# Half of the result blocks loaded into buffers outside the expert weights, one buffer per block

## The chip, the cores and the metric

The kernel runs on one core of a Trainium2 chip. The metric is the device time of one execution in microseconds (us); the time of the kernel before is the median of three runs, 806.97 us (805.11, 806.97 and 813.48). The core has a matrix engine (PE), a vector engine (DVE), an activation engine (ACT), GpSimd (POOL) and SyncE (SP). SP, ACT and POOL issue DMAs, which all run on the core's 16 DMA engines.

## The reference

Input is x of 16 batches x 256 tokens x 128 values, f32. The layer has two halves:

```
x = x + ga * attention_and_mlp(layernorm(x) * (1 + ca) + sa)
h = layernorm(x) * (1 + cb) + sb
scores  = sigmoid(h @ gate_w.T);  ids = top 4 of (scores + e_bias), of 32 experts
topk_w  = scores[ids] / sum(scores[ids])
out[t]  = sum over the 4 experts e of  topk_w * ((silu(h @ w1[e]) * (h @ w3[e])) @ w2[e])
x = x + gb * out
```

The change touches only the last two lines: the sum over the four expert results of each token, its product with gb, and the addition to x.

## The kernel before, in words

Attention, the dense MLP and the routing run first, batch after batch. For each of its four experts a token's row is scattered to `xs` in device memory, sorted by expert, and the rows are then worked off in 192 tiles of 128 rows by the **expert loop**: 48 steps (`XSTEPS`) of four tiles. The batches fall into two parts: tiles of batches 0 to 11 come first (`FIRST_PART`), 32 steps, then those of batches 12 to 15, 16 steps.

In a step SP loads four tiles (`load_pair`, L478, started by `load_four`, which waits at L491 until a buffer of two steps ago is free), PE transposes them (L1282), multiplies by w1 and w3 (L1290, weights in `w13`, which lies in the tensor `BIAS`), ACT and DVE form silu(g)*u (L939, L1818), PE transposes (L1299) and multiplies by w2 (L1308, weights in `w2e`), and DVE weights the result and puts it into one of 64 slots of `YQ` (L1832, L1834). Each of the four slots counts up the semaphore `y_ev`. POOL scatters the slots to `ys` in device memory (L739), 128 rows of 512 bytes each, 128 scatters in all; the first 96 hold everything of batches 0 to 11. Their landings count the semaphores `yst0` to `yst3`. In `ys` the four results of a token lie side by side, so a batch is one block of 512 KB, 4 KB for each partition and token pair.

**The end of the kernel**, which the change is about, is the loop over the 16 batches (blocks) b that stands on four engines at once, each taking them in the order 0 to 15:

- SP, L510 to L520: after its last load for the expert loop it waits until `y_ev` says that the last slot is written, then for the scatters that hold the first 12 blocks, and loads block after block into a buffer `G[b % 10]`. From block 12 on it also waits for the last scatters (L517), from block 10 on for the buffer's release (`g_free`, L519).
- PE, L1352 to L1367: waits for the end of the loop too. It adds the four results for 11 of the 16 blocks (all but 2, 5, 8, 11 and 14) by four accumulating matmuls with the identity, 256 columns each, in f32; each is recorded as two. For the blocks 0 to 5 of its own it then waits for its own matmuls before it releases the buffer (L1365).
- DVE, L1865 to L1886: for a PE block it multiplies the PSUM bank by gb (L1870) and adds it to X (L1886). For the other five it adds the four results itself (L1877, L1879), multiplies (L1883) and adds to X (L1886).
- ACT, L986 to L990: sends each finished batch of X to the output, 128 KB a batch, and waits for all of them.

The ten buffers `G` are six in `w13` and four in `w2e`: both hold expert weights that the loop reads until its last step. Other memory of that size is idle in the loop: the modulation rows `moda` and gate rows `gates[0]` of the first half, the buffer `early` and the hidden buffer `hid[0]`; some of them serve as rows for the scatter to `xs` and are free once that has landed, which SP waits for at L503.

Of the kernel before, what the change touches and what calls it, by code (L numbers as in the profile page):

```python
# [28 lines left out]
NB, SEQ, D = 16, 256, 128  # L29
# [5 lines left out]
NE, TOPK, INNER = 32, 4, 96  # L35
# [16 lines left out]
XG = 4  # L52
# [4 lines left out]
XSTEPS = XTILES // XG  # L57
# [22 lines left out]
def build(nc, x, ln1_w, Wq, Wk, Wv, rel_bias, scale, Wo, ln2_w, W1, W2, gate_w, w1, w3, w2, e_bias, c, wmod,  # L80
          onehot, out):
    ctx = ExitStack()
    with ctx:
        def sb(name, shape, dt=F32):
            return ctx.enter_context(nc.sbuf_tensor(name, shape, dt))

        def sem(name):
            return ctx.enter_context(nc.semaphore(name))

        def dram(name, shape):  # L90
# [11 lines left out]
        ident = sb("ident", [P, P])  # L102
# [26 lines left out]
        gates = [modb[:, i * NB * D:(i + 1) * NB * D].rearrange("p (b d) -> p b d", b=NB) for i in range(2)]  # L129
        moda_flat = modb[:, 2 * NB * D:]  # L130
# [7 lines left out]
        w13 = BIAS[:, :, :].rearrange("p u w -> p (u w)")  # L138
        w2r = sb("w2e", [P, NE, D])
# [9 lines left out]
        early = sb("early", [P, 2 * SEQ + UW])  # L149
# [34 lines left out]
        hid_flat = [hid[i][:, :, :].rearrange("p c t -> p (c t)") for i in range(2)]  # L184
# [55 lines left out]
        yidx = sb("yidx", [P, SLOTS + YGROUP], I32)  # L240
        tag = [sb(f"tag{i}", [P, XG, 2]) for i in range(4)]
        G = [f[:, i * TPB * TOPK * D:(i + 1) * TPB * TOPK * D].rearrange("p (t k d) -> p t k d", t=TPB, k=TOPK)
             for f, n in ((w13, 6), (w2r[:, :, :].rearrange("p e d -> p (e d)"), 4)) for i in range(n)]
        acc = [V[0][:, :, :, :].rearrange("p t h s -> p (t h s)")[:, i * SEQ:(i + 1) * SEQ].rearrange(
            "p (t d) -> p t d", t=TPB) for i in range(4)]

        def summed_on_pe(b):
            return b % 3 != 2
# [3 lines left out]
        names = """ld_c ld_wm ident_ready ld_x0 ld_x ld_w ld_v ld_b ld_e pool_c pool_s pool_n   # L252
# [9 lines left out]
             cnt_pe zero_ready zero_done  x_rows0 x_rows1 x_rows2 x_rows3  t_ready wr_t ld_t   # L262
            xt_pe xt_ev gu_pe sg_act a_dve at_pe at_act y_pe y_ev xg_ev yz yst0 yst1 yst2 yst3 pad_ready pad_done settled
             acc_s sum_s acc_ready ost0 ost1 ost2 ost3 ks_pe scat0 scat1 scat2 scat3 scat4 scat5 scat6 scat7 h2_copies""".split()
        names += [f"g_rows{i}" for i in range(len(G))] + [f"g_free{i}" for i in range(NB - len(G))]
        s = {n: sem(n) for n in names}
        block = ctx.enter_context(nc.Block())

# [4 lines left out]
        def bank(b, n=512, m=0):  # L273
            return PS[:, b, m:m + n]
# [90 lines left out]
        def tok(buf, b, t=0, n=1):  # L365

            return buf[:, bass.ds(b * TPB + t, n), :]
# [6 lines left out]
        def _(sp):  # L374
# [132 lines left out]
            with sp.Fori(early_fours, XSTEPS // 4 - 1) as four:  # L507
                load_four(four * 4)

            sp.wait_ge(s["y_ev"], XG * (XSTEPS + 2))  # L510
            ysv = ys[0:YROWS, :].rearrange("(b p t k) d -> b p (t k d)", b=NB, t=TPB, p=P)
            for b in range(NB):
                r = b % len(G)
                if b in (0, FIRST_PART):
                    slots = (FIRST_PART if b == 0 else NB) * TPB * TOPK
                    for g in range(SLOTS // 16):
                        sp.wait_ge(s[f"yst{g}"], 16 * 16 * (slots // SLOTS + (1 if g < slots % SLOTS // 16 else 0)))  # L517
                if b >= len(G):
                    sp.wait_ge(s[f"g_free{r}"], 1)  # L519
                sp.dma_start(G[r].rearrange("p t k d -> p (t k d)"), ysv[b]).then_inc(s[f"g_rows{r}"], 16)  # L520


        @block.gpsimd
# [470 lines left out]
        def _(pe):  # L994
# [13 lines left out]
            for j in range(2):  # L1008
                last = pe.transpose(bank(0, NB, j * NB), mrow[:, 3 + j, :], ident[0:NB, 0:NB])
# [137 lines left out]
            with pe.Fori(0, 5) as two:  # L1147
                b = two * 2 + 1
# [205 lines left out]
            n = 0  # L1354
            for b in range(NB):
                if summed_on_pe(b):
                    r = b % len(G)
                    pe.wait_ge(s[f"g_rows{r}"], 16 * (b // len(G) + 1))
                    if n >= 4:
                        pe.wait_ge(s["acc_s"], n - 4 + 1)  # L1360
                    for k in range(TOPK):
                        last = pe.matmul(bank(n % 4, SEQ), ident[:, :], G[r][:, :, k, :], start=(k == 0), stop=(k == TOPK - 1))
                    last.then_inc(s["ks_pe"], 1)
                    if b + len(G) < NB:
                        pe.wait_ge(s["ks_pe"], n + 1)  # L1365
                        pe.sem_inc(s[f"g_free{r}"], 1)
                    n += 1  # L1367


# [1 line left out]
        def _(dve):  # L1371
# [227 lines left out]
            with dve.Fori(0, 5) as two:  # L1599
                b = two * 2 + 1  # L1600
# [259 lines left out]
            for n in range(4):  # L1860
                i = XSTEPS - 4 + n
# [2 lines left out]

            n = m = 0  # L1865
            for b in range(NB):
                r, o = b % len(G), acc[b % 4]
                if summed_on_pe(b):
                    dve.wait_ge(s["ks_pe"], n + 1)
                    dve.tensor_tensor(o, bank(n % 4, SEQ).rearrange("p (t d) -> p t d", t=TPB),  # L1870
                                      gates[1][:, b:b + 1, :].to_broadcast([P, TPB, D]), ALU.mult).then_inc(s["acc_s"], 1)
                    n += 1
                    dve.wait_ge(s["acc_s"], n)
                else:
                    g = G[r]
                    dve.wait_ge(s[f"g_rows{r}"], 16 * (b // len(G) + 1))
                    dve.tensor_tensor(g[:, :, 0:2, :], g[:, :, 0:2, :], g[:, :, 2:4, :], ALU.add).then_inc(s["sum_s"], 1)  # L1877
                    dve.wait_ge(s["sum_s"], 3 * m + 1)
                    dve.tensor_tensor(o, g[:, :, 0, :], g[:, :, 1, :], ALU.add).then_inc(s["sum_s"], 1)  # L1879
                    dve.wait_ge(s["sum_s"], 3 * m + 2)  # L1880
                    if b + len(G) < NB:
                        dve.sem_inc(s[f"g_free{r}"], 1)
                    dve.tensor_tensor(o, o, gates[1][:, b:b + 1, :].to_broadcast([P, TPB, D]), ALU.mult).then_inc(s["sum_s"], 1)  # L1883
                    m += 1
                    dve.wait_ge(s["sum_s"], 3 * m)
                dve.tensor_tensor(tok(X, b, 0, TPB), tok(X, b, 0, TPB), o, ALU.add).then_inc(s["acc_ready"], 1)  # L1886
# [26 lines left out]
```

## Time and profile before

| | |
|---|---|
| median of three runs | 806.97 us |
| time of the profiled execution | 804.88 us |
| its span, first to last instruction | 802.9 us |
| mean granted clock of PE | 0.834 |
| PE busy | 546.2 us (68%) |
| DVE busy | 451.6 us (56%) |
| POOL busy | 388.8 us (48%) |
| ACT busy | 339.6 us (42%) |
| moved over the span | 71.36 MB, mean 89 GB/s |

The profiled execution is 2.1 us below the median; 2.0 us of its time lie outside the span. Busy shares are means over the whole kernel and say little about its end, which is the last 32 us. All places in time below are microseconds from the start of this span.

### The profile page before, as it was taken

What the parts mean: (1) busy time and instruction counts of PE and PEld (TensorE: products, weight loads), DVE (VectorE), ACT (ScalarE), POOL (GpSimd) and SP (SyncE); (2) the same over time, 40 slices, a digit from 0 to 9 for tenths busy, and PEclk for the clock granted to TensorE, in tenths of its full rate; (3) what the DMA queues carried; (4) which work ended last, traced back from release to release, by engine and by line L of the source; (5) the groups of instructions that cost most, each with busy time, mean ns of one, the idle gap of its engine ahead of it and who ended that gap; (6) DMA issues with size and microseconds to landing.
All of it is one profiled execution on the core that took longest, in us unless ns stands there. A gap on an engine that the chain in (4) does not pass through costs nothing.

```text
span 802.9 us, 16756 instructions
## 1 busy us (share of the span) xinstructions
PE 546.2 (68%) x4634; PEld 443.8 (55%) x4635; DVE 451.6 (56%) x1516; ACT 339.6 (42%) x757; POOL 388.8 (48%) x621
## 2 busy tenths in 40 slices
PE   2489999999997775745553123875664865858747
PEld 0256666666666653635543012775554855858735
DVE  5879888898884756454265440533423434434537
ACT  0268888888884443313223112433323433323200
POOL 5566666666520546373373456263553454443520
PEclk9779999999999997676785556878986878978859
DMA  7997000000005101010011553354332232323159
GB/s 233 317 271 195 1 0 0 0 0 2 2 2 158 42 34 49 27 59 27 33 53 41 86 151 103 103 88 110 98 94 74 70 96 76 89 79 96 57 205 334
DMA packets 85307, 71.36 MB, mean 89 GB/s; under 512 B 11017, under 2 KB 78832, under 8 KB 85248
## 3 DMA queue, kind: packets, MB, share of 16 engines
q1 hardware_dynamic: 67392, 48.04, 21.6%
q0 software_dynamic: 8192, 17.84, 6.8%
q10 hardware_dynamic: 9664, 4.79, 2.0%
q8 instruction: 25, 0.41, 0.2%
q14 instruction: 34, 0.28, 0.1%
HBM read 41.12 MB, written 32.66 MB: 92 GB/s over the span
## 4 chain that ended last, share of the span: by engine, by line
PE 39%; another core or an unknown queue 20%; issue 14%; DVE 11%; ACT 10%; DMA 3%; DVEq 2%; POOL 1%; ACTq 0%; POOLq 0%; SPq 0%
PE PS L1290 9%; PE PS L1058 4%; PE PS L1079 4%; PE PS L1176 3%; DVE L L1441 2%; PE PS L1032 2%; PE PS L1308 2%; ACT hid L857 2%; DMA BIAS<-ys 2%; PE PS L1095 2%; PE PS L1282 2%; PE PS L1084 1%; PE PS L1164 1%; PE PS L1061 1%
## 5 line engine op out<-in xcount | busy, mean ns | idle before, releaser
L739 POOL DMA_INDIRECT ys<-YQ,yidx x128 | 122.9, 960 | 155.0 <-DVE yidx L1834 121.6
L1290 PE MATMUL PS<-BIAS,V 128*128 x384 | 93.2, 397 | 81.8 <-ACT YT L947 43.0
L1832 DVE SCALAR_TENSOR_TENSOR YQ<-PS,tag,YQ 128x128 f32 x192 | 67.4, 351 | 141.6 <-remote 56.1
L1441 DVE TENSOR_TENSOR L<-PS,BIAS 128x768 f32<-128x768 f32 x128 | 116.7, 950 | 19.9 <-PE PS L1061 17.3
L1290 PEld LDWEIGHTS PS<-BIAS,V 128*128 128x128 f32 x384 | 76.9, 230 | 90.4 <-issue 90.4
L787 ACT ACTIVATE PR<-L 128x768 f32<-128x768 f32 x128 | 105.3, 841 | 41.0 <-DVE L L1441 31.3
L719 POOL DMA_INDIRECT xs<-YQ,posi x64 | 62.2, 972 | 83.8 <-issue 45.0
L1176 PE MATMUL PS<-w2s,hid 128*128 128x128 f32 x256 | 49.0, 369 | 59.1 <-ACT hid L857 34.9
L939 ACT ACTIVATE L<-PS 128x384 f32<-128x384 f32 x48 | 23.6, 491 | 152.0 <-remote 71.7
L1176 PEld LDWEIGHTS PS<-w2s,hid 128*128 128x128 f32 x256 | 45.2, 274 | 63.9 <-ACT hid L857 38.0
L719 POOL DMA_INDIRECT xs<-modb,posi x48 | 46.3, 965 | 39.4 <-DVE posi L1707 24.9
L1058 PE MATMUL PS<-YQ 32*128 32x256 f32 x512 | 59.7, 439 | 2.7 <-DVE L L1441 1.7
L857 ACT ACTIVATE hid<-PS 128x1024 f32<-128x1024 f32 x16 | 16.4, 1023 | 80.7 <-remote 62.7
L1079 PE MATMUL PS<-PR,V 128*32 128x256 f32 x512 | 41.8, 396 | 3.8 <-DVE YQ L1475 3.4
L1058 PEld LDWEIGHTS PS<-YQ 32*128 32x128 f32 x512 | 31.1, 188 | 19.5 <-issue 12.9
L1164 PE MATMUL PS<-RAW,w1s 128*128 128x256 f32 x128 | 38.4, 453 | 2.1 <-ACT RAW L853 1.9
L1061 PEld LDWEIGHTS PS<-YQ 32*128 32x128 f32 x512 | 38.2, 192 | 1.4
L952 ACT ACTIVATE V<-PS 128x512 f32<-128x512 f32 x48 | 28.6, 595 | 23.5 <-issue 14.5
L1061 PE MATMUL PS<-YQ 32*128 32x128 f32 x512 | 38.1, 276 | 0.0
L1282 PE MATMUL PS<-ident,PR 128*128 128x128 f32 x192 | 34.9, 315 | 0.9 <-issue 0.9
L1164 PEld LDWEIGHTS PS<-RAW,w1s 128*128 128x128 f32 x128 | 28.3, 233 | 7.6 <-ACT RAW L853 2.8
L1032 PE MATMUL PS<-wqkv,early 128*128 128x384 f32 x64 | 27.6, 558 | 5.9 <-DVE YQ L1432 3.6
(286 smaller groups left out, 1189.0 us busy)
## 6 DMA issues: line engine op xcount, KB each, us to landing
PR<-xs SPq DMA_DIRECT2D x192, 72.0 KB
BIAS<-ys SPq DMA_DIRECT2D x12, 512.0 KB, 9.5
xs<-pad_row SPq DMA_DIRECT2D x1, 4608.0 KB, 24.9
xs<-pad_row SPq DMA_DIRECT2D x57, 72.0 KB, 20.6
dist_rep<-dist_row SPq DMA_DIRECT2D x4, 768.0 KB, 7.9
X<-in_x ACTq DMA_DIRECT2D x4, 512.0 KB, 6.5
BIAS<-dist_rep SPq DMA_DIRECT2D x4, 512.0 KB, 8.0
modb<-mod_rows SPq DMA_DIRECT2D x2, 1024.0 KB, 9.1
```

The source lines that it names most:

```text
L719: pool.indirect_dma_start(out=xs, out_offset=bass.IndirectOffsetOnAxis(ap=posi[j][:, t * TOPK + k:t * TOPK + k + 1], axis=0), in_=ROWS[j][ ...
L739: pool.indirect_dma_start(out=ys, out_offset=bass.IndirectOffsetOnAxis(ap=yidx[:, n:n + 1], axis=0), in_=YQ[:, n * D:(n + 1) * D], in_offs ...
L787: act.activation(PR[u % 4][:, :], L[u % 2][:, :], ACT.Exp).then_inc(s["exp_done"], 1)
L1058: pe.matmul(bank(S_A + quad, SEQ), KT[par][r, 0:P], QM[par][r, j, :], start=True, stop=True)
L1061: last = pe.matmul(bank(S_A + quad, P, SEQ), KT[par][r, P:SEQ], QM[par][r, j, P:SEQ], start=True, stop=True)
L1079: pe.matmul(o, V[par][:, 0, h, :], pr[:, (j % 2) * HW:(j % 2) * HW + SEQ], start=True, stop=False, skip_group_check=True)
L1164: last = pe.matmul(bank(1 + ch // 2, SEQ, (ch % 2) * SEQ), w1s[:, ch * P:(ch + 1) * P], mT[n % 2], start=True, stop=True)
L1176: last = pe.matmul(bank(3 + 4 * (n % 2), P, t * P), hid[n % 2][:, ch, t * P:(t + 1) * P], w2s[:, ch, :], start=(ch == 0), stop=(ch == HID ...
L1282: last = pe.transpose(bank(buf % 2, P, j * P), xg[buf][:, j, 0:P], ident[:, :])
L1290: last = pe.matmul(bank(2 + 2 * par + j // 2, 2 * INNER, (j % 2) * 2 * INNER), xgT[par][:, j * P:(j + 1) * P], w13[:, bass.ds(e * (2 * INN ...
L1441: return dve.tensor_tensor(L[u % 2][:, :].rearrange("p (j w) -> p j w", j=2), PS[:, at:at + 2, 0:HW], BIAS[:, u, :].rearrange("p (j w) -> ...
L1832: dve.scalar_tensor_tensor(to, bank(6 + par, D, k * D), tag[buf][:, k, 0:1], to, ALU.mult, ALU.add)
```

## The change

The list of buffers becomes sixteen, one for each block: blocks 0 to 3 in `moda`, 4 and 5 in `gates[0]`, 6 in `early`, 7 in `hid[0]`, 8 to 13 in `w13`, 14 and 15 in `w2e`. SP's wait for the end of the expert loop moves behind the first eight loads; its waits for the scatters stay. The waits for and releases of buffers go. The sums, their order and the split between PE and DVE stay as they are.

```diff
         G = [f[:, i * TPB * TOPK * D:(i + 1) * TPB * TOPK * D].rearrange("p (t k d) -> p t k d", t=TPB, k=TOPK)
-             for f, n in ((w13, 6), (w2r[:, :, :].rearrange("p e d -> p (e d)"), 4)) for i in range(n)]
+             for f, n in ((moda_flat, 4), (gates[0].rearrange("p b d -> p (b d)"), 2), (early, 1), (hid_flat[0], 1),
+                          (w13, 6), (w2r[:, :, :].rearrange("p e d -> p (e d)"), 2)) for i in range(n)]
+        EARLY = 8
...
-            sp.wait_ge(s["y_ev"], XG * (XSTEPS + 2))
             ysv = ys[0:YROWS, :].rearrange("(b p t k) d -> b p (t k d)", b=NB, t=TPB, p=P)
             for b in range(NB):
-                r = b % len(G)
+                if b == EARLY:
+                    sp.wait_ge(s["y_ev"], XG * (XSTEPS + 2))
                 if b in (0, FIRST_PART):
                     slots = (FIRST_PART if b == 0 else NB) * TPB * TOPK
                     for g in range(SLOTS // 16):
                         sp.wait_ge(s[f"yst{g}"], 16 * 16 * (slots // SLOTS + (1 if g < slots % SLOTS // 16 else 0)))
-                if b >= len(G):
-                    sp.wait_ge(s[f"g_free{r}"], 1)
-                sp.dma_start(G[r].rearrange("p t k d -> p (t k d)"), ysv[b]).then_inc(s[f"g_rows{r}"], 16)
+                sp.dma_start(G[b].rearrange("p t k d -> p (t k d)"), ysv[b]).then_inc(s[f"g_rows{b}"], 16)
...
                 if summed_on_pe(b):
-                    r = b % len(G)
-                    pe.wait_ge(s[f"g_rows{r}"], 16 * (b // len(G) + 1))
+                    pe.wait_ge(s[f"g_rows{b}"], 16)
...
-                        last = pe.matmul(bank(n % 4, SEQ), ident[:, :], G[r][:, :, k, :], start=(k == 0), stop=(k == TOPK - 1))
+                        last = pe.matmul(bank(n % 4, SEQ), ident[:, :], G[b][:, :, k, :], start=(k == 0), stop=(k == TOPK - 1))
                     last.then_inc(s["ks_pe"], 1)
-                    if b + len(G) < NB:
-                        pe.wait_ge(s["ks_pe"], n + 1)
-                        pe.sem_inc(s[f"g_free{r}"], 1)
...
-                    g = G[r]
-                    dve.wait_ge(s[f"g_rows{r}"], 16 * (b // len(G) + 1))
+                    g = G[b]
+                    dve.wait_ge(s[f"g_rows{b}"], 16)
...
-                    if b + len(G) < NB:
-                        dve.sem_inc(s[f"g_free{r}"], 1)
```

## Rows read from the trace of the kernel before

**Rows 1.** The end by stretches: length, busy us by engine, PE clock, DMA share, GB/s
```profile
744.00:750.00 6.00, 5.96 (x46) 5.54 (x44) 4.04 (x19) 3.03 (x6) 2.87 (x3) 1.00 0.20 59
750.00:757.00 7.00, 6.22 (x44) 5.74 (x44) 4.54 (x21) 2.49 (x5) 3.84 (x4) 1.00 0.11 40
...
763.00:771.00 8.00, 2.07 (x8) 1.78 (x8) 4.88 (x24) 0.59 (x1) 0.11 (x1) 0.50 0.02 8
771.00:774.70 3.70, 0.00 (x0) 0.03 (x1) 0.00 (x0) 0.00 (x0) 2.88 (x3) 0.50 0.66 226
774.70:778.50 3.80, 3.75 (x8) 2.49 (x8) 0.01 (x1) 0.00 (x0) 0.96 (x1) 0.50 1.02 371
778.50:803.00 24.50, 18.85 (x80) 14.80 (x80) 18.19 (x42) 0.00 (x0) 0.00 (x0) 0.99 0.93 347
```

**Rows 2.** The chain of waits that ended last, from 770 us: start, us, what
```profile
770.91 3.65 DMA BIAS<-ys
...
774.70 3.76 PE PS L1362 x8
...
782.79 9.96 DMA BIAS<-ys
```

**Rows 3.** DMA in 771 to 803 us, by queue and by issue
```profile
q1 hardware_dynamic: 2304, 8.39, 66.5%
q10 hardware_dynamic: 4352, 2.10, 22.0%
```

**Rows 4.** SP's waits from 560 us on: waited for, us, times, longest
```profile
SPq L520 <- DVE yidx L1834: 26.1, 1, 26.1
SPq L520 <- PEq L1366: 5.0, 3, 1.9
```

**Rows 5.** Timeline of the end: start, us, engine, line, what
```profile
770.73 0.15 DVE L1834 TENSOR_TENSOR yidx<-yidx,tag 128x1 f32 x1
770.91 3.21 SPq L520 DMA_DIRECT2D BIAS<-ys  x6
...
780.81 1.96 PE L1362 MATMUL PS<-BIAS,ident 128*128 128x256 f32 x8
...
785.19 5.42 PE L1362 MATMUL PS<-w2e,ident 128*128 128x256 f32 x24 [0.30 <-PE PS L1362]
...
791.70 0.42 DVE L1870 TENSOR_TENSOR V<-PS,modb 128x256 f32<-128x256 f32 x1
...
792.49 0.41 DVE L1870 TENSOR_TENSOR V<-PS,modb 128x256 f32<-128x256 f32 x1
...
793.29 0.68 DVE L1877 TENSOR_TENSOR BIAS<-BIAS 128x512 f32<-128x512 f32 x1
...
795.26 0.42 DVE L1870 TENSOR_TENSOR V<-PS,modb 128x256 f32<-128x256 f32 x1
...
799.78 0.42 DVE L1886 TENSOR_TENSOR X<-X,V 128x256 f32<-128x256 f32 x1
```

**Rows 6.** POOL's timeline: the 96th scatter and the last
```profile
702.27 0.96 POOL L739 DMA_INDIRECT ys<-YQ,yidx  x1 [0.30 <-issue]
...
774.82 0.96 POOL L739 DMA_INDIRECT ys<-YQ,yidx  x1 [0.30 <-issue]
```

**Rows 7.** SP's waits at L517: duration, first and last start
```profile
L517 SPq EVENT_SEMAPHORE  x3: 28/28/28, 744.7 to 781.2; - x3
```

**Rows 8.** DMA queues in 744 to 757 us: packets, MB, share of 16 engines
```profile
q0 software_dynamic: 192, 0.39, 7.7%
q1 hardware_dynamic: 437, 0.22, 6.8%
q8 instruction: 1, 0.02, 0.5%
```

**Rows 9.** Chain of waits inside the expert loop, from 708 us
```profile
709.95 8.70 another core or an unknown queue
...
728.95 3.18 issue
```

More of the change, by code:

```diff
@@ L264, in build @@
              acc_s sum_s acc_ready ost0 ost1 ost2 ost3 ks_pe scat0 scat1 scat2 scat3 scat4 scat5 scat6 scat7 h2_copies""".split()
-        names += [f"g_rows{i}" for i in range(len(G))] + [f"g_free{i}" for i in range(NB - len(G))]
+        names += [f"g_rows{i}" for i in range(len(G))]
         s = {n: sem(n) for n in names}
@@ L1866, in _ @@
             for b in range(NB):
-                r, o = b % len(G), acc[b % 4]
+                o = acc[b % 4]
                 if summed_on_pe(b):
```

## The prediction

> **What bounds the kernel now.** I read the end from the coarse view inwards. In the busy times by stretch [rows 1] the reader should see two regimes. Up to 771 us the DMA engines are nearly idle (shares of 0.20 and 0.11 in 744 to 757 us, 0.02 in 763 to 771 us). From 774.7 us they are full (1.02, then 0.93), while PE works 18.85 us and DVE 18.19 us of 24.5. The chain of waits [rows 2] says the same: the loop's end is followed by 3.65 us of waiting for the first block to land, one block on PE, and later 9.96 us of waiting for a load into BIAS. The queues give the size [rows 3]: 8.39 MB of blocks, and the outputs, 16 of 128 KB, 2.10 MB, so 10.49 MB. From the loop's last DVE instruction, which ends at 770.88 us, to the last addition, at 799.78 + 0.42 = 800.20 us, it is 29.3 us [rows 5]. At the 371 GB/s of 774.7 to 778.5 us [rows 1] the 10.49 MB take 28.3 us. So the end is bound by DMA, with PE and DVE close below.
>
> Nothing but its place in the program keeps the loads back. SP waits 26.1 us in one piece for the last slot before its first load [rows 4]; it got there at 770.91 − 26.1 = 744.8 us, and its event row at L517 first stands at 744.7 us [rows 7]. The scatters that blocks 0 to 11 need were issued by 702.27 us [rows 6]: 32 of the 128 come after it.
>
> **The change part by part.**
>
> *Eight loads move ahead of the wait.* SP reaches them behind its last tile load, at about 744.8 us. Their condition, the first 96 scatters, has had over 40 us to land. Their 4.19 MB take 4.19/0.371 = 11.3 us, and with 3.65 us from issue to first landing [rows 2] they are in by about 760 us, 11 us before the loop ends. Every tile load of the loop is ahead of them in SP's own queue, so none is queued behind them. What does share the DMA engines with them are POOL's scatters and instruction fetches [rows 8]: 192 packets of scatters and one fetch in 744 to 757 us. A scatter is waited for only by the last four blocks. The fetch is the one thing that could cost time: nothing if the engine has instructions in hand. The nearest rows for a fetch that is waited for are stalls of the loop that no other engine explains, 3.18 and 8.70 us [rows 9]; they are not proven to be fetches. I take zero, since PE ran 5.96 us of 6.00 and 6.22 of 7.00 in that stretch [rows 1] and a late foreign packet must first use up such reserves, and keep 3.2 us for the range. A gain here is excluded: the loop's order and its loads are untouched.
>
> *The other queue under full load.* The last scatter is issued at 774.82 us [rows 6], and SP passes a wait at L517 at 781.2 us [rows 7]: 6.4 us for 64 KB while the blocks fill the engines. The Trainium skill, DMA: Bandwidth & Descriptors, Queues, rings and completion order, says that each DMA engine takes turns between its queues packet by packet. By that rule a fetch would wait for about one foreign packet, estimated at 0.16 us (8.39 MB in 2304 packets [rows 3], at a sixteenth of 371 GB/s), and the allowance of 3.2 us would be nearly nothing; the trace shows that the scatters got through under load, but not at what wait per packet. The forecast is the same by both.
>
> *The first block is there at once.* PE waits for the same end of the loop (L1353), then finds its block. Before, it started 774.70 us, 0.13 us behind the landing at 774.57 [rows 2]. Now it starts at 770.88 + 0.15 = 771.03 us. PE's granted clock is 0.50, the lower level of 1.2 GHz, from 763 to 778.5 us, after a stretch in which PE worked only 2.07 us of 8; from 778.5 us it is 0.99, 2.4 GHz [rows 1]. It rose once PE had been busy through its first block. I let that happen again, so block 0 costs 3.76 us [rows 2] and ends at 774.79 us. Best case: the full level from the start, 1.81 us, a gain of another 1.95. Worst: two blocks at the lower level, 1.95 us lost.
>
> *Releases go.* Four times (blocks 0, 1, 3, 4) PE no longer waits for its own matmuls. A block there, as the one at 780.81 us, cost 1.96 us and then a gap [rows 5], but 5.42/3 = 1.81 us where three follow without a release [rows 5]. I take 1.81 us for all. SP's 5.0 us of waits for PE's releases [rows 4] go too, and DVE's releases, register-like instructions of no recorded cost.
>
> *The new sum.* It is the longer of three resources.
> - DMA: 8 blocks and all outputs, 4.19 + 2.10 = 6.29 MB. At 371 GB/s that is 17.0 us; started at 770.91 + about 2 us it ends near 790 us.
> - PE: 11 blocks, 3.76 + 10 x 1.81 = 21.9 us, from 771.03 to 792.9 us.
> - DVE: a PE block takes 792.49 − 791.70 = 0.79 us, a block of its own 795.26 − 793.29 = 1.97 us [rows 5]. Eleven and five of them are 18.5 us. It is fed by PE in order, so its finish follows PE's: block 13, PE's tenth, is ready at 792.9 − 1.81 = 791.1 us; DVE finishes it at 791.9, its own block 14 at 793.8, and block 15 with 0.45 + 0.42 at 794.7 us.
>
> The last addition so moves from 800.20 to 794.7 us, **5.5 us earlier**. What follows it, the last output, is the same work on then emptier DMA engines: 802.9 − 800.2 = 2.7 us before and after.
>
> *Who is late next?* Blocks 12 to 15 still wait for the last scatters. If those land at 781.2 us again, block 12 lands 3.65 us later, at 784.9 us, and PE wants it at 771.03 + 3.76 + 7 x 1.81 = 787.5 us. Block 15 lands behind the 2.1 MB of those four and the outputs of that time, say 8 more: 3.15 MB/0.371 = 8.5 us after 781.2, 789.7 us; PE wants it at 791.1 us. The margin is 1.4 us, and DVE, busy with block 14 until 793.8, gives another 0.9. So DMA is no longer the bound, but not far away.
>
> 5.5 us off the profiled 804.88 us gives 799.4; that execution is 2.1 us under the median of the three runs, and I keep to the median: 806.97 − 5.5 = **801.5 us**, 0.7% faster.
>
> **The rivals.**
>
> *A. Everything falls well.* PE gets the full level at once: 11 x 1.81 = 19.9 us, block 13 ready at 771.03 + 18.1 = 789.1 us, end at 792.8 us, a gain of 7.4 us: 799.6 us. For it: little, the clock was 0.50 in the 15 us before. It needs the loop's last step to raise it.
>
> *B. The early loads take back part of it.* 4.19 MB in 744.8 to 760 us delay one fetch or scatter that somebody waits for: 3.2 us lost [rows 9], net 2.3, 804.7 us. Or the same price is paid at the end, where 3.65 us of waiting for a DMA now hide whatever PE or DVE have to fetch for the new section. For it: unexplained stalls exist in the loop. Against: only one fetch falls into the window [rows 8].
>
> *C. Slower.* The place is the same, the one fetch of that stretch [rows 8]; the price is the long stall of 8.70 us [rows 9] laid on the loop, whose last three steps pass results from engine to engine with nothing to spare. 801.5 + 8.7 = 810.2 us, 0.4% slower. It decides as soon as the stall is over 5.5 us. Against it: that stall came with no bulk traffic on the DMA engines, so bulk traffic is not what makes it.
>
> *D. The change does not do what it says.* If the first scatters' wait were not satisfied until the last landings, or DMA stayed the bound through the last four blocks, the gain would be that of the releases alone, and in a DMA-bound end that is nothing: 807 us. Against: the count of scatters [rows 6].
>
> The Trainium skill, Runtime: NRT & Kernel Launch, Instruction fetch mechanics, speaks for B and C: fetches go by DMA, a taken branch out of the window forces a wait, while straight code is mostly hidden. The loops on DVE and PE end just there; no row here names the engine that a fetch is for.
>
> **How the numbers follow.** Chances: forecast 0.62, A 0.13, B 0.14, C 0.06, D 0.05. The range goes from A less the 1.9 us by which the lowest of the three runs lies under the median, 799.6 − 1.9 = 797.7, to B with a microsecond of spread, 805.8; outside are C, D and a little at the low end. A measurement of this kernel can tell about 1%, 8.1 us. Faster by more means below 798.9 us: the low half of A, and the part of the forecast where the runs or a clock that rises early add 2.6 us; 0.19. Slower by more, above 815.0, needs C twice or a bad set of runs: 0.05. The rest, 0.76, is within 1%.
>
> **What would show it.** In the changed trace: eight loads issued from about 744.8 us and a DMA share near 1 until 757; PE's first L1362 within 0.3 us of the last slot; its first block at about 3.76 us, later ones at 1.81 without gaps; no DMA as releaser in the last 30 us; last addition about 23.8 us after the loop's end instead of 29.3; the loop's end itself where it was, to a microsecond. A wrong prediction would show as a later loop end, a PE that stands between 771 and 775 us, or a load that still lands last.

## The result, and the profile after

Timed beside the kernel before, in 20 executions of each: median 805.67 us against 812.95 us, ratio 0.9884, 95% interval 0.9844 to 0.9924. Two later comparisons gave 0.9927 (0.9901 to 0.9953; 623.35 against 629.28 us) and 0.9902 (0.9878 to 0.9925; 623.98 against 629.16 us). In these two the same programs take 180 us less, of which more at the end. The forecast was 801.5 us, 0.7% faster. There are two kinds of sets of runs: the **long sets**, in which the kernel before takes 807 to 813 us (the comparison of the prediction, and early_twice, pe_ahead, pe_ahead12 and warm12), and the **short sets**, in which it takes 629 us (all the others). In the long sets the executions of one kernel spread by 3 to 4%, and the ratios leave out each kernel's slowest executions; so I compare the end between landmarks inside each trace. The **end section** runs from the last slot (end of the last yidx instruction) to the end of the last addition to X.

The profiled execution took 804.11 us (span 802.3 us), only 0.8 us less than the profiled one of before. It came to its last tile load 3.7 us later (748.13 against 744.46 us), in code that the change does not touch, so the two executions as wholes do not show the change. Its stretches, columns as in [rows 1]:

```profile
750.00:757.00 7.00, 6.94 (x52) 6.50 (x51) 4.54 (x22) 2.95 (x7) 2.88 (x3) 1.00 0.97 379
757.00:763.00 6.00, 3.89 (x30) 3.46 (x29) 3.52 (x16) 1.28 (x3) 4.65 (x5) 1.00 0.83 333
763.00:771.00 8.00, 1.64 (x11) 1.45 (x10) 2.19 (x11) 0.59 (x1) 3.04 (x4) 0.62 0.08 33
...
779.00:803.00 24.00, 17.51 (x80) 14.74 (x79) 18.01 (x42) 0.00 (x0) 1.02 (x2) 0.99 0.74 243
```

The DMA engines are full where they were idle (0.97 against 0.11 in 750 to 757 us), with PE busy 6.94 of 7.00 us beside them. In the end section their share is 0.74 instead of 0.93.

Its timeline, as in [rows 5]:

```profile
748.47 2.99 SPq L520 DMA_DIRECT2D modb<-ys  x6
...
775.29 0.15 DVE L1830 TENSOR_TENSOR yidx<-yidx,tag 128x1 f32 x1
775.47 10.39 SPq L520 DMA_DIRECT2D BIAS<-ys  x6
...
775.54 8.62 PE L1361 MATMUL PS<-modb,ident 128*128 128x256 f32 x32 [3.41 <-issue]
...
785.91 1.22 SPq L520 DMA_DIRECT2D w2e<-ys  x2
...
796.77 1.99 PE L1361 MATMUL PS<-w2e,ident 128*128 128x256 f32 x8 [2.26 <-DMA w2e<-ys]
...
799.26 0.42 DVE L1880 TENSOR_TENSOR X<-X,V 128x256 f32<-128x256 f32 x1
```

The first load goes out right behind the last tile load, PE starts 0.10 us behind the last slot, and the section takes 799.68 − 775.44 = **24.24 us** instead of 29.32. Most of the 5.08 us is the start: PE's first sum comes 0.10 us behind the last slot where it came 3.82 us behind it. At the section's end PE stands 2.26 us for block 15. The chain of waits, as in [rows 2], and SP's waits, as in [rows 4], say why:

```profile
779.36 5.63 DMA ys<-YQ,yidx
...
786.38 10.35 DMA w2e<-ys
...
796.77 2.01 PE PS L1361 x8
```

```profile
SPq L520 <- DVE yidx L1830: 23.0, 1, 23.0
SPq L519 <- DMA ys<-YQ,yidx: 7.4, 1, 7.4
```

The last scatter is issued 3.92 us after the last slot and takes 5.63 us to land; SP waits 7.4 us for it before block 12, and block 15 then needs 10.35 us. Its last packets show one reason. The blocks (queue q1) beside the instruction fetches (q8) in 794.0 to 794.6, 794.6 to 795.6 and 795.6 to 796.2 us:

```profile
q1 hardware_dynamic: 4, 0.01, 5.1%
...
q8 instruction: 1, 0.02, 5.9%
...
q1 hardware_dynamic: 2, 0.00, 4.7%
```

In the middle microsecond no packet of the blocks moved, but one fetch of 16 KB, which kept one DMA engine busy for 0.95 us (5.9% of sixteen); then came the block's last packet. bufs_only, the other trace in which PE waited over 2 us for block 15, has such a fetch in the same place; in the other traces of the changed kernel it came after the block's last packet. So about 1 us of the late landing is the fetch. That it stood ahead of the last packet on the same DMA engine is inferred from the order; the profile does not name the engine.

From 775 to 803 us the queues moved, as in [rows 3]:

```profile
q1 hardware_dynamic: 1152, 4.19, 44.2%
q10 hardware_dynamic: 4352, 2.10, 25.2%
```

Half the blocks, the same outputs.

### The profile page after: what moved, and what is told of

Its sections match the earlier page's. It is cut to its first block, busy times and chain, and to the rows that moved or that the text cites. A ratio compares the mean times of both kernels' runs of the same rounds, so it can differ in the third digit from the quotient of the medians.

```text
span 802.3 us, 16750 instructions
## 1 busy us (share of the span) xinstructions
PE 544.9 (68%) x4634; PEld 445.2 (55%) x4635; DVE 452.1 (56%) x1516; ACT 339.8 (42%) x757; POOL 388.7 (48%) x621
## 4 chain that ended last, share of the span: by engine, by line
PE 37%; another core or an unknown queue 23%; DVE 12%; issue 11%; ACT 10%; DMA 3%; DVEq 2%; POOL 1%; POOLq 0%; SPq 0%; ACTq 0%
PE PS L1290 8%; PE PS L1058 4%; PE PS L1079 4%; PE PS L1176 3%; DVE L L1437 2%; PE PS L1032 2%; PE PS L1308 2%; ACT hid L857 2%; PE PS L1282 2%; PE PS L1095 2%; PE PS L1084 1%; PE PS L1061 1%; DMA w2e<-ys 1%; PE PS L1164 1%
## 5 line engine op out<-in xcount | busy, mean ns | idle before, releaser
L1308 PE MATMUL PS<-w2e,YT 96*128 x192 | 28.1, 294 | 6.4 <-DVE yidx L1830 6.4
```

## The experiments

**Theory** before these runs: before, the end was bound by loading 16 blocks after the loop; the early start removes that, and PE and DVE, with the last blocks' landing close by, bound it now; the loop does not notice the early loads. **Rival R1:** the releases and PE's waits for its own matmuls were the cost. **Rival R2:** the early loads change the expert loop.

All landmarks and times in one table, the long sets first, the short ones from before_again on; the **loop stretch** is the time from SP's last tile load to the last slot. The landmarks are of one trace each.

| kernel | before, us (median) | this, us (median) | ratio (95%) | loop stretch | end section |
|---|---|---|---|---|---|
| before | | | | 26.43 | 29.32 |
| after | 812.95 | 805.67 | 0.988 (0.984-0.992) | 27.32 | 24.24 |
| early_twice | 812.62 | 805.79 | none given | 27.32 | 24.72 |
| pe_ahead | 812.62 | 804.30 | 0.999 (0.993-1.005) | 27.35 | 22.34 |
| pe_ahead12 | 812.62 | 802.16 | 0.990 (0.987-0.994) | 25.91 | 18.71 |
| warm12 | 812.62 | 807.29 | 0.995 (0.991-0.999) | 26.26 | 22.61 |
| before_again | | 630.97 | | 20.40 | 29.94 |
| after_again | 629.28 | 623.35 | 0.993 (0.990-0.995) | 20.26 | 23.96 |
| after_third | 629.16 | 623.98 | 0.990 (0.988-0.993) | 20.29 | 24.36 |
| bufs_only | 629.28 | 629.68 | 0.999 (0.997-1.002) | 20.26 | 29.67 |
| early_reuse | 629.28 | 625.06 | 0.993 (0.990-0.995) | 20.27 | 25.62 |
| early12 | 629.28 | 622.30 | 0.989 (0.986-0.991) | 19.75 | 23.68 |
| late_out | 629.16 | 623.39 | 0.991 (0.989-0.994) | 20.25 | 24.36 |
| pe_ahead12_again | 629.16 | 619.79 | 0.985 (0.982-0.987) | 19.64 | 20.26 |

**The same two kernels again.** No edit.

> The changed kernel once more, for the spread and a second trace. Main theory (the end is no longer bound by loading all 16 blocks): from the last slot's yidx instruction to the last addition 24.2 us as in its first trace, against 29.3 us before; the total 5 us shorter. Rival (the early loads also change the expert loop): the stretch from SP's last tile load to the last slot differs from the 26.4 us of before by more than 2 us again and again (27.3 us in the first trace of after).

> The changed kernel again, timed beside the kernel before on the same chip: ratio 0.991 to 0.993 (5.5 us less of 629 or of 812 us), end section 24.0 to 24.2 us, stretch of the loop's end 20.3 us without the unexplained stalls, 27.3 us with them.

> The kernel before once more, for a second trace: end section 29.3 to 29.7 us; if it runs where the expert loop has unexplained stalls (total about 807 to 813 us), the stretch from the last tile load to the last slot tells what eight early loads cost: 26.4 us again would mean 0.9 us (three traces with them had 27.3), 27.3 us would mean nothing.

In the short sets the end section falls by 5.6 to 6.0 us, the median time by 5.2 and 5.9 us (by 6.2 and 4.6 us going by the ratios): the whole gain lies in the end section. The question that before_again was to decide stayed open, since it ran in a set without the long stalls. In its trace the end of before is not bound by DMA from end to end. A load keeps PE waiting only once, for block 0:

```profile
600.32 3.75 PE L1362 MATMUL PS<-BIAS,ident 128*128 128x256 f32 x8 [8.30 <-DMA BIAS<-ys]
604.23 2.91 PE L1362 MATMUL PS<-BIAS,ident 128*128 128x256 f32 x8
```

That is 4.1 us behind the last slot; from there PE's and DVE's own work with their waits for each other fills the section. So of the 6.0 us between before_again and after_again 4.0 are the wait for the first landing.

The chain of after_again shows what bounds the changed kernel:

```profile
593.52 5.92 PE PS L1361 x16
...
599.46 0.44 DVE V L1866
...
616.95 0.43 DVE X L1880
```

PE's first two blocks, then DVE alone: it has no idle time over 0.15 us from 599.46 to its end at 617.38 us, 17.92 us. after_third, early_twice, early12 and late_out have the same 17.9 us. Between them the end section differs only by PE's first two blocks, 5.6 to 6.6 us, that is, by when PE's clock rises.

**bufs_only.** The wait stands first again:

```diff
-        EARLY = 8
+        EARLY = 0
```

> Sixteen buffers and no releases, but SP's wait for the last slot stands ahead of the first load as before. Main theory: the loads of all 16 blocks still start after the loop, so the end section stays at 28.5 to 29.5 us and the total within 1 us of before. Rival (the releases and PE's waits for its own matmuls were the cost): the end section falls to about 24 us and the total by 5 us.

No gain: 629.68 against 629.28 us, end section 29.67 us. R1 falls as a cause by itself. The chain is DMA nearly from end to end:

```profile
602.16 5.84 DMA ys<-YQ,yidx
...
609.40 15.56 DMA w2e<-ys
...
625.00 2.01 PE PS L1361 x8
```

**early_reuse.** Early loads, but ten buffers and the releases as before (edit against the kernel before):

```diff
-             for f, n in ((w13, 6), (w2r[:, :, :].rearrange("p e d -> p (e d)"), 4)) for i in range(n)]
+             for f, n in ((moda_flat, 4), (gates[0].rearrange("p b d -> p (b d)"), 2), (early, 1), (hid_flat[0], 1),
+                          (w13, 2)) for i in range(n)]
...
-            sp.wait_ge(s["y_ev"], XG * (XSTEPS + 2))
...
+                if b == 8:
+                    sp.wait_ge(s["y_ev"], XG * (XSTEPS + 2))
```

> Eight early blocks as in the changed kernel, but ten buffers only (two of them in the expert weights): blocks 10 to 15 reuse the buffers of blocks 0 to 5 behind the releases, and PE waits for its own matmuls four times. Main theory: the early start is what counts; the end section is 24.2 us plus up to 4 x 0.3 us of PE waits, 24.2 to 25.5 us, the total 4 to 5 us below before. Rival (releases): 28 us or more, total like before.

End section 25.62 us, 1.5 us above the mean of after_again and after_third. The median time is 1.7 us above that of after_again, the ratios are equal (0.9928 and 0.9927), so the time does not resolve it. The early start with the releases in place brings 4.0 to 4.3 us (29.67 and 29.94 less 25.62). The missing releases bring up to 1.5 us more, and only together with it: alone they bring nothing (bufs_only). The chain shows PE's blocks one by one, with a gap behind each release:

```profile
596.87 3.77 PE PS L1364 x8
...
600.77 2.59 PE PS L1364 x8
...
603.49 1.98 PE PS L1364 x8
...
605.61 1.98 PE PS L1364 x8
...
607.87 2.18 PE PS L1364 x9
```

PE comes to its fifth block 11.0 us after its first, in after_again after 9.2 us. DVE waits for PE twice more, 0.46 and 0.22 us, so about 0.7 us of the 1.5 are the releases for certain. The rest lies in the first two blocks (6.48 us, against 5.90 and 6.29), where the rise of the clock, which comes at another place in each trace, cannot be told from the release.

**early12.** Twelve early blocks. Four more buffers are made of memory that the loop leaves idle (the dense weights, the rows of the first half, the second half of `hid[1]` with the first of `YT`), by allocating neighbours together (those lines of the edit are left out here):

```diff
...
-                          (w13, 6), (w2r[:, :, :].rearrange("p e d -> p (e d)"), 2)) for i in range(n)]
-        EARLY = 8
+                          (wpack, 1), (hpack, 1), (rpack, 1), (ypack[:, 2 * SEQ:6 * SEQ], 1), (w13, 4)) for i in range(n)]
+        EARLY = 12
```

> Twelve blocks, all whose scatters are in by then, get buffers outside the expert weights and are loaded early; four remain. Main theory with the trace's 2.26 us of PE waiting for block 15: that wait goes, PE and DVE run through, the last addition comes about 1.0 us earlier than in the changed kernel: end section 23.2 us. If DMA were still the bound it would shorten by the 2.1 MB at 371 GB/s, 5.7 us, to 18.5 us. Rival (early loads disturb the loop): twelve disturb more than eight, the stretch from SP's last tile load to the last slot grows by 1 us or more over that of the changed kernel.

23.68 us. DMA as the bound would have given 18.5. Against the changed kernel in the short sets (23.96, 24.36) it is 0.3 to 0.7 us, not 1.0, and even that is not the edit's: PE's first four blocks took 9.07 us here, 9.35 and 9.75 us there, the same differences. No PE wait for block 15 stood in the traces of the short sets, so there was nothing to remove. The loop stretch did not grow.

**early_twice.** Each early block is loaded twice, and PE and DVE wait for the second landing (those two lines are left out here):

```diff
                 if b == EARLY:
+                    for again in range(EARLY):
+                        sp.wait_ge(s[f"g_rows{again}"], 16)
+                        sp.dma_start(G[again].rearrange("p t k d -> p (t k d)"), ysv[again]).then_inc(s[f"g_rows{again}"], 16)
```

> The changed kernel, but each of the eight early blocks is loaded a second time behind its first load (4.19 MB more), so the DMA engines are full for about 23 us from the last tile load on, to the loop's end. Main theory (bulk loads do not slow the loop): the stretch from the last tile load to the last slot stays at 20.3 us as in the four traces of the first set (or 26.4 to 27.3 us where the loop has unexplained stalls), within 0.5 us; the loads of blocks 8 to 11 start up to 3 us later, the end section grows by no more than that. Rival (they do): the stretch grows by 1 us or more.

Over its loop stretch:

```profile
745.00:772.20 27.20, 15.49 (x108) 14.11 (x106) 14.14 (x65) 6.11 (x12) 11.49 (x12) 0.80 0.87 343
```

The DMA engines are busy to 0.87 of 27.2 us and the stretch is 27.32 us, what it was in the changed kernel with half the traffic. In the short sets it is 20.26 and 20.40 us without an early load (bufs_only, before_again), 20.25 to 20.29 with eight (four traces) and 19.6 to 19.8 with twelve. There R2 falls. In the long sets it does not fall altogether: before had 26.43 us, all three traces with eight early blocks 27.3. The difference sits in one wait of DVE, in before and in after:

```profile
762.88 0.35 DVE L1832 SCALAR_TENSOR_TENSOR YQ<-PS,tag,YQ 128x128 f32 x1 [4.61 <-PE PS L1308]
...
767.43 0.35 DVE L1828 SCALAR_TENSOR_TENSOR YQ<-PS,tag,YQ 128x128 f32 x1 [5.32 <-remote]
```

It ends 18.4 us behind the last tile load in before and 19.3 us in after; from there to the last slot it is 8.0 us in both. In early_twice and pe_ahead DVE waits 5.42 and 5.32 us there. What ends this wait is not recorded. Its length does not grow with the traffic (early_twice), but with a single trace of before in the long sets a cost of up to 0.9 us for any early load there is neither shown nor excluded. The two kernels with twelve early blocks had 25.91 and 26.26 us, with waits of other lengths in other places.

**pe_ahead.** PE waits for what its banks need instead of the last slot:

```diff
-            pe.wait_ge(s["y_ev"], XG * (XSTEPS + 2))
+            pe.wait_ge(s["at_act"], XSTEPS + 2)
```

> The changed kernel without PE's wait for the last slots: the first sums only need PSUM banks 0 to 3, which the loop has left once ACT has read the last transposed product, and that is what PE waits for. PE starts about 3.3 us ahead of the last slot instead of 0.10 us behind it. If PE and DVE bound the end: end section 20.5 to 21 us (24.0 less 3.3). If the landing of the last blocks bounds it, as PE's 2.26 us of waiting for block 15 in the first trace of the changed kernel says: block 15 lands no earlier than before, the end section stays at 22.5 to 24 us and PE waits for a load at its end.

22.34 us, between the two, and the waits name the second cause:

```profile
PE PS L1361 <- DMA BIAS<-ys: 1.9, 1, 1.9
PE PS L1361 <- DMA w2e<-ys: 1.7, 1, 1.7
```

Of the 3.5 us by which PE was ahead, 3.6 went into waiting for two of the last blocks. The timing alone could not have told: the ratio is 0.999, while the median is 8.3 us under that of before, with a spread of 19 us.

**pe_ahead12.** Both edits.

> Both: twelve early blocks, and PE starts about 3.3 us ahead of the last slot. Only four blocks remain to be loaded, so PE should not wait for a load: end section 20.5 us (early12 had 23.7), total 3 us under early12 and 10 us (1.6%) under the kernel before. If DMA bounds the end here too: 22 us or more.

> Twelve early blocks and PE ahead of the last slot, the fastest so far, once more: end section 18.7 us, which is DVE's own work of 18.5 us for the 16 blocks, so 10.6 us below before and 5.3 us below the changed kernel: ratio to before 0.983 where before takes 629 us, 0.987 where it takes 812 us.

It is the fastest version of its set both times: 0.990 and 0.985. In the first execution PE waits 1.3 us for block 15, which DVE, busy without a gap, does not notice; in the second it waits for no load. The end sections miss both expectations, 18.71 where I had said 20.5 and 20.26 where I had said 18.7. The difference is mostly the clock. Stretches around the last slot, first execution, then second:

```profile
763.00:767.40 4.40, 4.40 (x20) 3.85 (x19) 2.78 (x15) 0.00 (x0) 0.53 (x1) 0.76 0.04 15
767.40:771.00 3.60, 3.60 (x18) 3.19 (x17) 3.43 (x10) 0.00 (x0) 2.84 (x3) 1.00 0.34 112
```

```profile
588.70:592.20 3.50, 3.50 (x11) 2.78 (x10) 2.12 (x11) 0.00 (x0) 1.92 (x2) 0.50 1.03 416
592.20:596.00 3.80, 3.80 (x17) 3.28 (x16) 2.28 (x6) 0.00 (x0) 2.87 (x3) 0.88 0.29 97
```

In the first, the sums followed two products of the loop without a break and the clock went from the lower to the full level among them (0.76, then 1.00). In the second, it stayed at the lower level until past the last slot. PE's first four blocks in the two, 7.78 and 9.23 us:

```profile
763.65 7.78 PE L1366 MATMUL PS<-modb,ident 128*128 128x256 f32 x32
```

```profile
588.72 9.23 PE L1366 MATMUL PS<-modb,ident 128*128 128x256 f32 x32
```

That is 1.45 us, about the whole difference of 1.55. Where the clock had risen early, DVE ran from the last slot to the end without a gap: its own work, forecast at 18.5 us, bound the end at 18.7.

**warm12.** early12 with eight matmuls of 256 columns, whose result nobody reads, before PE's wait for the last slot:

```diff
+            pe.wait_ge(s["g_rows0"], 16)
+            for k in range(8):
+                pe.matmul(bank(0, SEQ), ident[:, :], G[0][:, :, k % TOPK, :], start=True, stop=True)
             pe.wait_ge(s["y_ev"], XG * (XSTEPS + 2))
```

> Twelve early blocks, and PE runs eight matmuls of 256 columns with a result that nobody reads ahead of its wait for the last slots, so that it is busy in the 3.3 us before its first sum. If the lower level of the clock costs what I took for it (3.76 us for block 0 instead of 1.81), the first two sums take 3.6 to 4.0 us instead of 5.6 and the end section is 21.8 to 22.2 us instead of 23.7. If DVE alone bounds the end from block 1 on (it ran without a gap from there in the second trace of the changed kernel), the same 1.9 us are gained, since DVE waits for PE only twice. If the clock does not rise from it: 23.7 us.

```profile
773.37 4.86 PE L1360 MATMUL PS<-modb,ident 128*128 128x256 f32 x16
778.07 7.07 PE L1369 MATMUL PS<-modb,ident 128*128 128x256 f32 x32
```

The sums run at the full level from the first on: 7.07 us for four blocks (9.07 in early12). But the extra matmuls, at the lower level themselves for half of their time, ran past the last slot, and the first sum came 1.0 us behind it instead of 0.1; so 1.1 us of 2.0 were left (22.61 against 23.68, a long set against a short one). Real sums in that place, as in pe_ahead12, get both.

**late_out.** No output until block 15 is in:

```diff
+            act.wait_ge(s["g_rows15"], 16)
             for b in range(NB):
                 act.wait_ge(s["acc_ready"], b + 1)
```

> The changed kernel, but ACT sends no finished batch before block 15 has landed. If the outputs' share of the DMA engines is what made block 15 land 10.35 us after its issue (my estimate was 8.5 us for the last four together), it now lands in 7 us or less, PE does not wait for it and the last addition comes about 1 us earlier, 23.2 to 23.7 us after the last slot; the outputs then trail: 15 x 128 KB cannot be done 2.6 us after the last addition, the total is not shorter. If the late landing has another cause (the blocks wait for the last scatter and then need their time), block 15 lands as late as in the changed kernel, 21.3 us after the last slot.

The blocks in w2e land 5.7 us after their issue (median of the two), 7.1 in after_third in the same set; first fence late_out, second after_third:

```profile
w2e<-ys SPq DMA_DIRECT2D x2, 512.0 KB, 5.7
```

```profile
w2e<-ys SPq DMA_DIRECT2D x2, 512.0 KB, 7.1
```

So the outputs do hold up the last blocks, by about 1.4 us (one trace without them; after_again and early_twice have 7.0 with them). It did not matter here, since PE did not wait for block 15 in either kernel: 24.36 us both. Sixteen outputs held back until 610.02 us, 8.4 us before the last addition, cost nothing: the time is 623.39 against 623.98 us.

## Why the prediction was right, and where it was off

- **The bound of before**: only partly right. "Bound by DMA, with PE and DVE close below" gives the size, but the early start did not gain by sparing bytes: 3.7 of the 5.1 us (long set) and 4.0 of the 6.0 us (short set) are the wait for the first landing, which the prediction had too. Behind it, PE waited for loads 0.46 and 0.63 us in the trace of before, and not at all in before_again. With the releases gone and the loads late (bufs_only) the chain is DMA, at 29.67 us. So the bounds were within a microsecond of each other.
- **Early loads cost the loop nothing**: right in the short sets, by bufs_only against four traces with eight early blocks (20.26 against 20.25 to 20.29 us). In the long sets, where the forecast was made, the loop stretch was 0.9 us longer in all three traces, for a reason that is not shown; early_twice shows that it does not grow with the bytes. Rivals B and C at their prices (3.2 and 8.7 us) did not occur there. What spoke against C, that its stall came with no bulk traffic, was loose: the DMA share was 0.29 from 710 to 718.6 us, though far from full. The other half of B, a fetch that costs at the end, did occur in the first trace, at about 1 us. Rival D did not: SP's first load came 0.35 us behind its last tile load.
- **PE starts with the last slot, block 0 at the lower clock level**: right; 0.10 us behind it, and DVE got block 0 3.57 us after the last slot in the first trace and 3.89 us in after_again (3.91 forecast, 0.15 + 3.76). How long the lower level lasts differs: the first two blocks took 5.2 to 6.6 us in the three traces of the changed kernel and in early_twice (5.57 forecast).
- **Releases**: the prediction saw the gap behind a released block [rows 5] and left it out of the sum: it set 0.15 us a block against them, 0.6 us in all. In early_reuse the blocks follow each other at 2.1 to 2.3 us instead of 1.81, and the end section is 1.5 us longer, of which 0.7 us are the releases for certain.
- **The new sum**: 23.8 us for the end section (794.7 − 770.9), measured 24.24, 23.96 and 24.36. The number is right, its path is not. The prediction let DVE follow PE to the end, 11 blocks at 1.81 us. The traces show DVE waiting for PE at the first two blocks only, and then 17.9 us of its own work without a gap (but for block 15 in the first trace). DVE was the next bound; that both paths give nearly the same time here (0.15 + 3.76 + 1.81 + 17.75 = 23.5 us by the forecast's own terms) is luck.
- **Who is late next**: this step failed in the first trace and held in three others. Block 15 was forecast 18.8 us after the last slot; it landed after 17.9, 17.8 and 19.2 us in after_again, after_third and early_twice, and PE did not wait for it, but after 21.3 us in the first trace. The last scatter landed within the forecast (9.6 us after the last slot, 10.3 forecast). The 781.2 us behind that forecast was only the moment when SP came by, having just issued block 11 at 780.78 us, so the landing could be earlier. The last four blocks then took 796.73 − 784.99 = 11.7 us, 9.2 to 9.3 in the other three, where 8.5 was forecast. Of the excess in the first trace about 1 us is the fetch; the rest is open. PE's 2.26 us of waiting cost the end about 1.0 us, as DVE was busy with block 14 until 797.9 us in any case.
- **Rival A**, the clock: the full level from the first sum on did not happen in the changed kernel, but it is real, as warm12 and the two executions of pe_ahead12 show, 1.5 to 2.0 us.
- **The size**: 5.5 us forecast, 5.9 and 5.2 us between the medians of the short sets, 7.3 us between those of the long one. The ratio there (0.9884) corresponds to 9.4 us with 6.2 at the near end of its interval. The traces show 5.1 us in the end section and 0.9 us lost in the loop stretch; the surplus is in no trace. With a spread of 3 to 4% between executions I take it for scatter, but this is argued, not shown.
- **The absolute time**: 801.5 us stood on a median of three, 806.97, that was 6.0 us under the median of twenty. For that reason the measured 805.67 us lies at the upper edge of the range, 0.1 us inside. That it lies inside is luck: with the 5.5 us that were forecast it would have been 812.95 − 5.5 = 807.5 us, outside.

## What to carry to other kernels

When a wait of one engine stands ahead of a loop of loads, ask of each load what it alone needs: here eight blocks were complete 40 us earlier, and idle memory was enough to take them. Reusing buffers cost nothing while the loads came late and 0.7 to 1.5 us when they came early. The gain of an early load is first of all the time to its first landing, here 3.7 to 4.0 us, which nothing else covers. After a bound is removed the next edit follows from the new first waits: PE's start ahead of the last slot brought 1.9 us with eight early blocks, where it waited 3.6 us for the last of them, and 3.4 to 5.0 us with twelve; the upper figure holds about 1.5 us of the clock. And compare two ends only after taking out what the clock did at their start: the 0.3 to 0.7 us between early12 and the changed kernel are nothing else.

## What the runs showed of the hardware that was not expected

**The same program takes 629 us in some sets of runs and 812 us in others.** As far as the record tells, the chip does not decide it. The long set of early_twice, pe_ahead, pe_ahead12 and warm12 ran on chip number 13, and so did, five minutes later, the short set of before_again, after_third, late_out and pe_ahead12_again; the other short set ran on chip number 8. Part of the difference is in waits that no recorded event ends; over the expert loop of the kernel before, in the long set:

```profile
ACT L L939 <- remote: 71.7, 11, 8.9
DVE YQ L1832 <- remote: 56.1, 11, 10.0
ACT YT L947 <- remote: 18.2, 4, 8.5
```

The traces of the short sets have such waits only one at a time (in 300 to 600 us: before_again one of 4.7 us, after_third two of 3.0 and 3.5 us, bufs_only three of 5.0 to 5.7 us). What ends them is in no trace; instruction fetches are not shown to be it, and it stays open, as does what changed between the sets.

**The clock depends on what came directly before.** PE ran the same four sums in 7.07, 7.78, 9.07, 9.23 and 10.10 us (warm12, the two executions of pe_ahead12 with early12 between them, early_twice), as the 1.2 GHz level ended before them, or sooner or later within them.

**A fetch of 16 KB kept one DMA engine busy for 0.95 us**, and where it came ahead of the last packet of a 512 KB load, the load landed that much later (first trace and bufs_only).
